# Experts' rows weighed at PSUM and scattered with accumulation onto the shared output, instead of gathered in a last stage

## Chip, cores and metric

One core of a Trainium2 chip. The metric is the device time of one execution in microseconds (us); the core has five engines (TensorE, VectorE, ScalarE, GpSimd, which the profile calls POOL, and SyncE or SP, which only issues DMAs), SBUF for tiles and PSUM for the results of matmuls. All data are fp32; matmuls take pairs of fp32r halves (high and low part), three products for one.

## The reference

4096 tokens of 512 features. A state-space scan gives x1; then come the experts, the part that matters here:

```
logits = xt @ gate_w ; probs = softmax(logits) ; top_p, top_i = top_k(probs, 2)
for k in 0, 1:                       # every token goes to two experts of 8
    pos = running count of the tokens of this expert and this k
    keep = pos < 640                 # tokens beyond 640 are dropped
    y = gelu(x @ w1[e] + b1[e]) @ w2[e] + b2[e] + gelu(x @ wd[e]) @ wu[e]
    out += y * keep * top_p[:, k]
sh = gelu(xt @ sw1 + sb1) @ sw2 + sb2 + gelu(xt @ swd) @ swu
out = x1 + layernorm(out + 0.2 * sh)
```

where xt is the layer-normalised x1, w1 is 512x2048 and w2 2048x512. The two experts of a token differ, so within one expert no token stands twice.

## The kernel before, in words

The program has four stages, with a barrier of all engines between them: `prepare`, `mix` (the scans; beside them the shared expert's output for 28 of the 32 tiles of 128 tokens, stored to sh_d), `experts` and `combine`.

`experts` (L1011) first does the shared expert's last four tiles beside the router. The router ends with 64 pairs of comparisons on VectorE (L1531, L1533) that TensorE multiplies into a table, slot_tok: which token stands in which of an expert's 1280 slots. An empty slot names token 0. Then 8 experts follow, each in three blocks of 2, 4 and 4 tiles of 128 slots (EB). A block has 17 steps j. In step j TensorE makes the hidden rows (`up(j)`, 12 matmuls to psH), ScalarE applies gelu, VectorE splits the result into hh and hl (L1413 to L1421), and TensorE multiplies these with W2 into psY (`down(j)`), always one step behind `up`. Step 0 is the low-rank part (L1, L2). At a block's end VectorE evicts psY with the bias b2 to yst (L1436), and only after that, its order being fixed, splits step 0 of the next block; `down(0)` waits for it (L1628). yst has two tiles, so the third eviction waits until the first is stored. SP stores the tiles to y_d (L1186), one row for each slot.

Beside this the rows of coming blocks are gathered by POOL with indirect DMAs (`gather`, L1339) from xt_d into two xrow tiles and turned by TensorE at steps 2, 6, 10 and 14 of the block before (FRONT). A gather waits until the turn of its tile two before (s_T). In an expert's third block the next expert's weights come in: SP loads 36 pieces through four raw tiles (L1159), ScalarE rounds each to its high part (`convert_chunk`, from step 2 on, L1238), POOL subtracts for the low part (`lows`, L1334), which frees the raw tile. The last pieces are done after the block has ended. The order on POOL is written out by hand: gathers of blocks 1 and 2, `slots` (a wait for the new indices), gathers of block 0 of the next expert, then its 36 `lows`. All of it is one in-order queue, as is each other engine's.

`combine` (L1695) takes the tokens in 16 groups of two tiles through a ring of six buffers. POOL gathers each token's two rows from y_d (64 indirect DMAs, L1740), SP loads sh_d and x1_d, ScalarE weighs the first row (L1751), VectorE adds the second and 0.2 times the shared row (L1777, L1782), takes the statistics (L1786, L1789) and the scale; ScalarE normalises (L1759), VectorE adds x1 (L1803), SP stores out (L1719).

Of the kernel before, what the change touches and what calls it, by code (L numbers as in the profile page):

```python
# [17 lines left out]
F32 = mybir.dt.float32  # L18
# [20 lines left out]
TG, NG = 2, NS // 2  # L39

# [333 lines left out]
def mix(nc, sem, const, early, x, dt_d, dtx_d, bc_d, xT_d, w, ws_d, lgT_d, x1_d, xt_d, sh_d):  # L374
# [6 lines left out]
    with ExitStack() as ctx:  # L381
# [49 lines left out]
        s_bias = sem("b_biases_in")  # L431
# [153 lines left out]
        def _(act):  # L585
# [94 lines left out]
            for g in range(END):  # L680
# [31 lines left out]
        def _(dve):  # L712
# [50 lines left out]
            def shared_out(b, t):  # L763
                dve.wait_ge(s_mm2, (b + 1) * J)
                dve.wait_ge(s_bias, 32)
# [4 lines left out]
                nc.vector.tensor_tensor(yst[t][:, :], psS[t][:, :], b2bc[:, :], ALU.add).then_inc(s_yev, 1)  # L770
# [237 lines left out]
TRAIL = 2  # L1008


def experts(nc, sem, const, w, ws_d, lgT_d, x1_d, xt_d, sh_d, y_d):  # L1011
# [7 lines left out]
    wgt, row_g, lg = const["wgt"], const["row_g"], const["lg"]  # L1019
    with ExitStack() as ctx:  # L1020
# [5 lines left out]
        L1h, L1l = sb("L1h", [P, DT, P], F32R), sb("L1l", [P, DT, P], F32R)  # L1026
        L2 = sb("L2", [L3, D], F32R)
        X = [(sb(f"X{n}h", [P, DT, r], F32R), sb(f"X{n}l", [P, DT, r], F32R)) for n, r in (("a", 512), ("b", 512))]
# [5 lines left out]
        yst = [sb(f"yst{q}", [P, D]) for q in range(2)]  # L1034
# [3 lines left out]
        graw = sb("graw", [P, DT, E])  # L1038
        rs1, nm1 = sb("rs1", [P, NT]), sb("nm1", [P, NT])
        slot_tok = sb("slot_tok", [P, E * ST])  # L1040
        idx = sb("idx", [P, ST], I32)
# [4 lines left out]
        U, ones = sb("U", [P, P], F32, rt), sb("ones", [P, P], F32, rt)  # L1046
        m8, r8, w8 = sb("m8", [P, NT], F32, rt), sb("r8", [P, NT], F32, rt), sb("w8", [P, E], F32, rt)
        mx, pos = sb("mx", [P, K, NT], F32, rt), sb("pos", [P, K, NT], F32, rt)
        tok, tok_f = sb("tok", [P, NT], I32, rt), sb("tok_f", [P, NT], F32, rt)

        count_i = RA[:, :, :, :].rearrange("p k t e -> p (k t e)").bitcast(I32)[:, 0:P]
        count_f = U

# [6 lines left out]
        X.append((sb("Xch", [P, DT, 256], F32R), sb("Xcl", [P, DT, 256], F32R)))  # L1060
# [13 lines left out]
        s_yst = [sem(f"c_y_stored{q}") for q in range(2)]  # L1074
# [27 lines left out]
        def expert(e, k):  # L1102
            o, n = EB[k]
            return dict(B=e * 3 + 1 + k, t0=e * ST + BT + o, th=e * (ST // 2) + (BT + o) // 2, n=n,
                        gathered=True)
# [40 lines left out]
        y_v = y_d.rearrange("(e j p) d -> e p j d", e=E, j=ST)  # L1146

        @block.sync
        def _(sp):
# [33 lines left out]
            def store(at, dest):  # L1183
                for t in range(at["n"]):
                    pass_gate(sp, s_yev, at["t0"] + t + 1, g_sp)
                    sp.dma_start(dest(t), yst[t % 2][:, :]).then_inc(s_yst[t % 2], 16)  # L1186

            def store_shared(b):
                store(shared(b), lambda t: sh_d[bass.ds(b * (BT * P) + t * P, P), :])
# [698 lines left out]
```

## Time and profile before

| | |
|---|---|
| three runs | 3653.09, 3645.42, 3647.03 us; median 3647.03 |
| profiled execution, its own time | 3653.11 us |
| its span, first to last instruction | 3651.4 us |
| mean granted clock of TensorE | 0.917 |
| TensorE busy | 3143.7 us, 86% |
| VectorE, ScalarE, POOL busy | 51%, 38%, 43% |
| bytes moved by DMA | 480.08 MB |
| stages by TensorE's work | mix to about 1430 us, experts to 3524, combine to the end |

Busy time is the time in which an engine has an instruction at work; matmuls overlap, so a matmul's own 0.39 us is more than its share of 0.23. An idle stretch is given in brackets ahead of an instruction, with what ended it. A landing is the moment at which the last of a DMA's 16 queues reports.

### The profile page before, as it was taken

What the parts mean: (1) busy time and instruction counts of PE and PEld (TensorE: products, weight loads), DVE (VectorE), ACT (ScalarE), POOL (GpSimd) and SP (SyncE); (2) the same over time, 40 slices, a digit from 0 to 9 for tenths busy, and PEclk for the clock granted to TensorE, in tenths of its full rate; (3) what the DMA queues carried; (4) which work ended last, traced back from release to release, by engine and by line L of the source; (5) the groups of instructions that cost most, each with busy time, mean ns of one, the idle gap of its engine ahead of it and who ended that gap; (6) DMA issues with size and microseconds to landing.
All of it is one profiled execution on the core that took longest, in us unless ns stands there. A gap on an engine that the chain in (4) does not pass through costs nothing. (4 is left out here: it accounts for less than half of the span.)

```text
span 3651.4 us, 45197 instructions
## 1 busy us (share of the span) xinstructions
PE 3143.7 (86%) x15190; PEld 2580.2 (71%) x15190; DVE 1856.8 (51%) x2762; ACT 1394.6 (38%) x2475; POOL 1583.1 (43%) x1459
## 2 busy tenths in 40 slices
PE   6445698988989987989999999999999999999960
PEld 3223477777777775778888888888888888888840
DVE  6489889998899881542232222222222222223238
ACT  7445576666766762311221312212213122131114
POOL 1067787978979873420320502304214033051025
PEclk8655699999999998979999999999999999999985
DMA  6848697796886946810321302203113022031039
GB/s 231 230 153 224 188 246 193 209 257 192 235 217 207 257 139 181 249 52 18 88 64 30 109 24 63 79 15 101 53 41 99 21 72 76 9 110 44 15 125 347
DMA packets 281672, 480.08 MB, mean 131 GB/s; under 512 B 30497, under 2 KB 106097, under 8 KB 281474
## 3 DMA queue, kind: packets, MB, share of 16 engines
q1 hardware_dynamic: 223104, 296.62, 27.9%
q0 software_dynamic: 56704, 180.38, 16.7%
q8 instruction: 133, 2.18, 0.2%
q10 hardware_dynamic: 1666, 0.36, 0.1%
q14 instruction: 65, 0.53, 0.0%
HBM read 380.18 MB, written 97.11 MB: 131 GB/s over the span
## 5 line engine op out<-in xcount | busy, mean ns | idle before, releaser
L1419 DVE CAST hh<-h 128x512 fp32r<-128x512 f32 (+1 forms) x400 | 159.2, 398 | 1301.5 <-ACT h L1271 1295.7
L1271 ACT ACTIVATE h<-c_psH,b1e 128x512 f32<-128x512 f32 (+1 forms) x384 | 237.2, 618 | 1356.2 <-PE c_psH L1590 1328.8
L818 POOL TENSOR_TENSOR u<-dtxs,Bt 128x512 f32<-128x512 f32 x512 | 667.3, 1337 | 168.6 <-DVE b_psA L722 145.2
L722 DVE TENSOR_TENSOR_SCAN b_psA<-b_psA,carry,u 128x512 f32<-128x512 f32 x512 | 657.0, 1283 | 61.5 <-ACT b_psA L595 56.4
L1339 POOL DMA_INDIRECT xrow<-xt_d,idx x80 | 89.2, 1116 | 1099.6 <-PE c_psT L1581 603.3
L1632 PE MATMUL c_psY<-W2h,hh 128*128 128x512 f32 x1344 | 534.3, 398 | 0.1
L926 PE MATMUL b_psY<-ident,pr 128*128 128x128 f32 x2048 | 343.5, 306 | 215.0 <-DVE pr L729 197.7
L1632 PE MATMUL c_psY<-W2h,hl 128*128 128x512 f32 x1344 | 526.0, 391 | 0.0
L1632 PE MATMUL c_psY<-W2l,hh 128*128 128x512 f32 x1344 | 525.4, 391 | 0.0
L926 PEld LDWEIGHTS b_psY<-ident,pr 128*128 128x128 f32 x2048 | 263.5, 155 | 299.5 <-DVE pr L729 247.3
L729 DVE TENSOR_TENSOR pr<-b_psA,Ct 128x512 f32<-128x512 f32 x512 | 354.3, 692 | 17.9 <-DMA Ct<-bc_d 0.2
L595 ACT ACTIVATE b_psA<-dts,A_neg 128x512 f32<-128x512 f32 x512 | 354.4, 692 | 16.1
L1334 POOL TENSOR_TENSOR W1l<-raw,W1h 128x512 fp32r<-128x512 f32 x128 | 204.7, 1599 | 294.4 <-ACT W1h L1238 294.2
L961 PE MATMUL b_psH<-Xh,w 128*128 128x512 f32 x896 | 318.1, 416 | 7.7 <-DMA w<-ws_d 7.7
L980 PE MATMUL b_psS<-w,hhs 128*128 128x512 f32 x896 | 295.2, 411 | 0.0
L1632 PEld LDWEIGHTS c_psY<-W2h,hl 128*128 128x128 f32 x1344 | 252.9, 188 | 54.8
L1632 PEld LDWEIGHTS c_psY<-W2h,hh 128*128 128x128 f32 x1344 | 253.7, 189 | 51.2 <-DVE hl L1421 4.2
L1632 PEld LDWEIGHTS c_psY<-W2l,hh 128*128 128x128 f32 x1344 | 253.6, 189 | 47.2 <-issue 0.2
L1421 DVE TENSOR_TENSOR hl<-h,hh 128x512 fp32r<-128x512 f32 (+1 forms) x400 | 246.7, 617 | 13.7
L1590 PE MATMUL c_psH<-Xbh,W1l 128*128 128x512 f32 x576 | 224.1, 389 | 0.0
L1590 PE MATMUL c_psH<-Xbh,W1h 128*128 128x512 f32 x576 | 224.1, 389 | 0.0
L1590 PE MATMUL c_psH<-Xbl,W1h 128*128 128x512 f32 x576 | 224.1, 389 | 0.0
(251 smaller groups left out, 5596.8 us busy)
## 6 DMA issues: line engine op xcount, KB each, us to landing
w<-ws_d POOLq DMA_DIRECT2D x224, 512.0 KB, 6.8
raw<-in_w SPq DMA_DIRECT2D x256, 256.0 KB, 2.8
Bt<-bc_d SPq DMA_DIRECT2D x64, 512.0 KB
Ct<-bc_d SPq DMA_DIRECT2D x64, 512.0 KB, 24.5
y_d<-yst SPq DMA_DIRECT2D x80, 256.0 KB
xn<-in_x SPq DMA_DIRECT2D x8, 1024.0 KB, 6.3
xT_d<-xnT SPq DMA_DIRECT2D x8, 1024.0 KB, 8.5
dt_d<-a_dt SPq DMA_DIRECT2D x8, 1024.0 KB, 9.5
```

The lines of the kernel that those rows point to most:

```text
L595: nc.scalar.activation(psA[g % 2][:, :], dts[s % 2][:, :], ACT.Exp, scale=A_neg[:, s % DT, n:n + 1]).then_inc(s_dA, 1)
L722: nc.vector.tensor_tensor_scan(psA[q][:, :], psA[q][:, :], u[g % U_RING][:, :], carry[:, k:k + 1], ALU.mult, ALU.add).then_inc(s_h, 1)
L729: nc.vector.tensor_tensor(pr[g % PR_RING][:, :], psA[g % 2][:, :], C_of(g), ALU.mult)\
L818: nc.gpsimd.tensor_tensor(u[g % U_RING][:, :], dtx[s % 2][:, :], Bt[n // TG][:, n % TG, :], ALU.mult)\
L926: last = nc.tensor.matmul(psY[:, t, :], pr[g % PR_RING][:, t * P:(t + 1) * P], ident[:, :], start=(n == 0 and t == 0), stop=False, is_tran ...
L961: last = nc.tensor.matmul(psH[:, :], a[:, d, :], v[:, d, :], start=(d == 0 and i == 0), stop=(d == DT - 1 and i == 2))
L980: last = nc.tensor.matmul(psS[t][:, :], a, v, start=False, stop=(j == FC and i == 2))
L1271: nc.scalar.activation(h32[:, 0:n * P], psH[j % 2][:, 0:n * P], ACT.Gelu, bias=b1[:, j - 1:j]).then_inc(s_gelu, 1)
L1334: nc.gpsimd.tensor_tensor(lo, view, hi.bitcast(F32), ALU.subtract).then_inc(s_wlo, 1)
L1421: nc.vector.tensor_tensor(hl[j % 2][a], h32[a], hh[j % 2][a].bitcast(F32), ALU.subtract)\
L1590: last = nc.tensor.matmul(out, a, b, start=(i == 0), stop=(i == n - 1))
L1632: last = nc.tensor.matmul(psY[t][:, :], a[j % 2][:, c], b, start=False, stop=(j == J - 1 and i == 2))
```

## The change

The last stage no longer gathers. The shared output, already times 0.2, is stored to acc_d instead of sh_d; each expert's rows, times their token's weight, are added onto acc_d by an indirect DMA that accumulates, 80 in all. `tail` takes `combine`'s place: it loads the sum and x1, normalises, adds, stores. For this:

- ScalarE prepares each yst tile with weight times b2 (`weigh_bias`, at steps 4, 6, 8, 10 of each block); the eviction is psY times the weight plus that. There are four yst tiles now; which block uses which, and when one is free again, is written in Y_TILE and Y_TURN. In an expert's first block tiles 0 and 1 come from the third and fourth scatter of the expert before.
- The weights are turned, stored to two columns in DRAM after the router, and gathered for each tile of slots, 128 of 4 bytes (`gather_weights`, POOL).
- Two tables instead of one: slot_g for gathers, slot_s for scatters, where an empty slot names a spare row of its own behind row 4096.
- POOL also stores the shared rows of the last block and issues the scatters. The first scatter of an expert waits for all those of the expert before, since two experts can have the same token; VectorE writes the new scatter indices at step 12 of the first block after the same wait.
- SP keeps only weights and b2.

```diff
+Y_TILE = ((0, 1), (2, 3, 0, 1), (2, 3, 0, 1))
+Y_TURN = ((0, 0), (0, 0, 1, 1), (1, 1, 2, 2))
+Y_USES = (3, 3, 2, 2)
+WEIGH_AT = (4, 6, 8, 10)
@@ mix: ScalarE, VectorE @@
+                if g == NU:
+                    act.wait_ge(s_bias, 32)
+                    nc.scalar.mul(b2bc[:, :], b2bc[:, :], SHARE).then_inc(s_b02, 1)
-                nc.vector.tensor_tensor(yst[t][:, :], psS[t][:, :], b2bc[:, :], ALU.add).then_inc(s_yev, 1)
+                nc.vector.scalar_tensor_tensor(yst[t][:, :], psS[t][:, :], SHARE, b2bc[:, :], ALU.mult, ALU.add)\
+                    .then_inc(s_yev, 1)
@@ experts: SP @@
             load_pieces(1, weights_of(0))
-            store_shared(SB - 1)
             bias2(0, expert(0, 0))
-            store_expert(0, 0)
-            store_expert(0, 1)
...
@@ experts: ScalarE @@
+            def weigh_bias(at, t):
+                if at["gathered"]:
+                    e, k = at["e"], at["k"]
+                    i, free = y_free(e, k, t)
+                    pass_gate(act, s_b2, (e + 2) * 16, g_act)
+                    pass_gate(act, s_wg[k], (e + 1) * EB[k][1] * 16, g_act)
+                    pass_gate(act, s_yst[i], free, g_act)
+                    scale = wsl[:, EB[k][0] + t:EB[k][0] + t + 1]
...
+                nc.scalar.mul(yst[i][:, :], b2bc[:, :], scale).then_inc(s_b2w, 1)
...
+            act.wait_ge(s_wT, 1)
+            nc.scalar.copy(weight_rows, psT[1][0:K * NT, 0, :]).then_inc(s_wTc, 1)
+            act.wait_ge(s_wTc, 1)
+            for k in range(K):
+                act.dma_start(w_d[k].rearrange("(r p) o -> r (p o)", p=P), weight_rows[k * NT:(k + 1) * NT, :])\
+                    .then_inc(s_wst, 16)
+            act.wait_ge(s_wst, K * 16)
@@ experts: POOL @@
+            def scatter(e, k):
+                at = expert(e, k)
+                if k == 0:
+                    pass_gate(pool, s_sidx, e + 1, g_pool)
+                    for i in range(4):
+                        pass_gate(pool, s_yst[i], added(e, i), g_pool)
+                for t in range(EB[k][1]):
+                    i = Y_TILE[k][t]
+                    pass_gate(pool, s_yev, at["t0"] + t + 1, g_pool)
+                    nc.gpsimd.indirect_dma_start(
+                        out=acc_d[:, :],
+                        out_offset=bass.IndirectOffsetOnAxis(ap=sidx[:, EB[k][0] + t:EB[k][0] + t + 1], axis=0),
+                        in_=yst[i][:, :], in_offset=None, bounds_check=T + SLOTS - 1,
+                        compute_op=ALU.add).then_inc(s_yst[i], 16)
...
             def steady(e, last=False):
-                for k in (1, 2):
-                    for t in range(EB[k][1]):
-                        gather(e, k, t)
...
+                gathers(e, 2, range(2))
+                scatter(e, 0)
+                gathers(e, 2, range(2, 4))
+                gather_weights(e, 2)
+                if not last:
+                    slots(e + 1)
+                    gathers(e + 1, 0, range(2))
+                    gather_weights(e + 1, 0)
+                scatter(e, 1)
+                if not last:
+                    for j in range(J):
+                        lows(e + 2, j)
+                    gathers(e + 1, 1, range(2))
+                scatter(e, 2)
+                if not last:
+                    gathers(e + 1, 1, range(2, 4))
+                    gather_weights(e + 1, 1)
@@ experts: VectorE @@
-                dve.wait_ge(s_b2, bias_count)
                 for t in range(n):
-                    after(dve, s_yst[t % 2], (at["th"] + t // 2) * 16)
-                    nc.vector.tensor_tensor(yst[t % 2][:, :], psY[t][:, :], b2bc[:, :], ALU.add).then_inc(s_yev, 1)
+                    dve.wait_ge(s_b2w, at["t0"] + t + 1)
...
+                    nc.vector.scalar_tensor_tensor(yst[i][:, :], psY[t][:, :], scale, yst[i][:, :], ALU.mult, ALU.add)\
+                        .then_inc(s_yev, 1)
...
+            def scatter_rows(e):
+                for i in range(4):
+                    pass_gate(dve, s_yst[i], added(e, i), g_dve)
+                v.tensor_copy(sidx[:, :], slot_s[:, bass.ds(e * ST, ST)]).then_inc(s_sidx, 1)
...
-                run(expert(e, 0), (e + 2) * 16, nxt=(expert(e, 1), X_OF[1]))
+                run(expert(e, 0), nxt=(expert(e, 1), X_OF[1]), extra={12: (lambda: scatter_rows(e),)})
@@ tail, in combine's place @@
+        @block.sync
+        def _(sp):
+            for g in range(NG):
+                sp.dma_start(y[g][:, :, :], rows(acc_d, g)).then_inc(s_y[g], 16)
+                sp.dma_start(x1r[g][:, :, :], rows(x1_d, g)).then_inc(s_x1[g], 16)
+        @block.gpsimd
+        def _(pool):
+            for g in range(NG):
+                pool.wait_ge(s_x, (g + 1) * G)
+                pool.dma_start(rows(out, g), y[g][:, :, :]).then_inc(s_out, 16)
+            pool.wait_ge(s_out, NG * 16)
```

In `tail` each of the 16 groups has its own tiles. ScalarE does the root and the normalising, VectorE `stats(g)`, `scale(g - 1)` and `residual(g - 2)` in turn, as before without the two weighted sums. The L1 tiles of step 0 have 104 columns now instead of 128, and some tiles of the router share space with one of the X tiles. VectorE gets four small operations on 80 columns after the router's table, one of them ahead of the indices.

## Rows read from the trace of the kernel before

**Rows 1.** Busy us by stretch, expert stage: engines, granted clock, DMA share, GB/s

```profile
1560.00:3524.00 1964.00, 1923.86 (x9300) 1622.40 (x9299) 541.48 (x1139) 422.09 (x755) 441.92 (x340) 0.98 0.18 55
```

**Rows 2.** The same view, last stage: the whole, and its middle

```profile
3531.00:3651.40 120.40, 0.00 (x0) 0.00 (x0) 87.27 (x192) 48.48 (x81) 75.81 (x64) 0.50 0.94 349
3535.00:3630.00 95.00, 0.00 (x0) 0.00 (x0) 72.29 (x159) 39.40 (x66) 71.27 (x61) 0.50 1.03 382
```

**Rows 3.** Lines of the last stage, VectorE: busy us, mean ns | idle before

```profile
L1777 DVE SCALAR_TENSOR_TENSOR d_y<-d_y,wgt 128x512 f32<-128x512 f32 x32 | 22.7, 749 | 31.1 <-ACT d_y L1751 16.3 <-DMA d_y<-y_d,row_g 14.3 <-issue 0.5
L1782 DVE SCALAR_TENSOR_TENSOR d_y<-d_sh,d_y 128x512 f32<-128x512 f32 x32 | 20.6, 685 | 0.0
...
L1786 DVE BATCH_NORM_STATS2 d_st<-d_y 128x6 f32<-128x512 f32 x32 | 20.4, 680 | 0.0
```

**Rows 4.** Waits of the expert stage: us in total, times, longest us

```profile
PE c_psY L1628 <- DVE hh L1416: 19.9, 9, 2.9
...
DVE yst L1436 <- DMA y_d<-yst: 31.8, 15, 3.2
```

**Rows 5.** DMA issues: KB each, median us from issue to landing

```profile
xrow<-xt_d,idx POOLq DMA_INDIRECT x80, 3.8
...
xt_d<-xrow SPq DMA_DIRECT2D x4, 256.0 KB, 2.0
```

**Rows 6.** Timeline of the seam before the last stage, and its end

```profile
3524.11 1.29 DVE L1436 TENSOR_TENSOR yst<-c_psY,b2bc 128x512 f32<-128x512 f32 x2 [3.49 <-PE c_psY L1632]
...
3527.02 1.29 DVE L1436 TENSOR_TENSOR yst<-c_psY,b2bc 128x512 f32<-128x512 f32 x2 [1.62 <-DMA y_d<-yst]
3531.05 0.38 SPq L1724 DMA_DIRECT2D d_sh<-sh_d  x1
...
3645.33 2.49 DVE L1803 TENSOR_TENSOR d_y<-d_y,d_x 128x512 f32<-128x512 f32 x4
```

**Rows 7.** Timeline of two turns to a new expert, engine by engine: start, us

```profile
1850.81 1.29 DVE L1436 TENSOR_TENSOR yst<-c_psY,b2bc 128x512 f32<-128x512 f32 x2 [2.53 <-DMA y_d<-yst]
...
1852.66 0.42 DVE L1416 TENSOR_TENSOR hh<-h,hl 32x256 fp32r<-32x256 f32 x1
...
1853.13 0.73 PE L1628 MATMUL c_psY<-L,hh 96*128 96x512 f32 x2 [2.38 <-DVE hh L1416]
...
1852.24 1.01 POOL L1339 DMA_INDIRECT xrow<-xt_d,idx  x1 [0.30 <-issue]
...
1849.67 0.38 ACT L1265 ACTIVATE h<-c_psH 96x256 f32<-96x256 f32 x1 [0.17 <-ACT b1e L1312]
...
1862.94 0.47 ACT L1271 ACTIVATE h<-c_psH,b1e 128x256 f32<-128x256 f32 x1 [2.15 <-PE c_psH L1590]
1865.78 0.47 ACT L1271 ACTIVATE h<-c_psH,b1e 128x256 f32<-128x256 f32 x1 [2.36 <-PE c_psH L1590]
...
3291.40 0.42 DVE L1416 TENSOR_TENSOR hh<-h,hl 32x256 fp32r<-32x256 f32 x1
...
3288.90 0.38 ACT L1265 ACTIVATE h<-c_psH 96x256 f32<-96x256 f32 x1
```

**Rows 8.** Busy us by stretch behind two turns; TensorE's gap at the second

```profile
1853.00:1860.00 7.00, 6.87 (x37) 6.20 (x38) 1.51 (x5) 1.25 (x3) 0.25 (x1) 0.76 0.57 181
1999.00:2006.00 7.00, 6.36 (x29) 5.06 (x28) 3.30 (x6) 2.32 (x6) 3.38 (x4) 1.00 0.60 173
...
1999.89 1.20 PE L1628 MATMUL c_psY<-L,hh 96*128 96x512 f32 x4 [0.64 <-issue]
```

**Rows 9.** Timeline of VectorE after the shared block

```profile
1571.06 1.32 DVE L1436 TENSOR_TENSOR yst<-c_psY,b2bc 128x512 f32<-128x512 f32 x2 [1.58 <-DMA sh_d<-yst]
```

**Rows 10.** Timeline from the end of a second block to POOL's first lows

```profile
1993.95 1.29 DVE L1436 TENSOR_TENSOR yst<-c_psY,b2bc 128x512 f32<-128x512 f32 x2 [3.66 <-PE c_psY L1632]
...
2004.88 1.60 POOL L1334 TENSOR_TENSOR L1l<-raw,L1h 128x192 fp32r<-128x192 f32 x2 [2.84 <-ACT L1h L1238]
```

More of the change, by code:

```diff
@@ L39 @@
 TG, NG = 2, NS // 2
+SHARE = 0.2
 def after(eng, sem, value):
@@ L1033, in experts @@
         xrow = [sb(f"xrow{q}", [P, D]) for q in range(2)]
-        yst = [sb(f"yst{q}", [P, D]) for q in range(2)]
+        yst = [sb(f"yst{q}", [P, D]) for q in range(4)]
         b2bc = sb("b2bc", [P, D])
@@ L1181, in rows @@
                     row_out(b, t)
[L1183 to L1189, printed above, removed]
-            def store_expert(e, k):
-                store(expert(e, k), lambda t: y_v[bass.ds(e, 1), :, EB[k][0] + t, :].rearrange("o p d -> (o p) d"))
             def bias2(e, at):
-                pass_gate(sp, s_yev, at["t0"], g_sp)
+                pass_gate(sp, s_b2w, at["t0"], g_sp)
                 sp.dma_start(b2bc[:, :], w["b2"][bass.ds(e, 1), :].rearrange("o d -> (o d)").partition_broadcast(P))\
@@ L1276, in run @@
                         extra[j]()
+                    if j in WEIGH_AT and WEIGH_AT.index(j) < n:
+                        weigh_bias(at, WEIGH_AT.index(j))
                     if wset is not None and j >= TRAIL:
@@ L1376, in _ @@
                 pool.wait_ge(s_xts[q], BT // 2 * 16)
+            store_shared(SB - 1)
             slots(0)
-            for t in range(EB[0][1]):
-                gather(0, 0, t)
-            def steady(e, last=False):
-                for k in (1, 2):
-                    for t in range(EB[k][1]):
-                        gather(e, k, t)
-                if last:
-                    return
-                slots(e + 1)
-                for t in range(EB[0][1]):
-                    gather(e + 1, 0, t)
-                for j in range(J):
-                    lows(e + 2, j)
+            gathers(0, 0, range(2))
+            pool.wait_ge(s_wst, K * 16)
+            gather_weights(0, 0)
+            gathers(0, 1, range(4))
+            gather_weights(0, 1)
+            def steady(e, last=False):
+                gathers(e, 2, range(2))
[15 more added lines that the diff above has]
+                    gather_weights(e + 1, 1)
             with pool.Fori(0, E - 1) as e:
@@ L1522, in expert_slots @@
                 pass_gate(dve, s_T, expert(e, 0)["t0"], g_dve)
[L1523 removed]
+                if not (isinstance(e, int) and e == 0):
+                    pass_gate(dve, s_wg[2], e * EB[2][1] * 16, g_dve)
+                v.tensor_copy(idx[:, :], slot_g[:, bass.ds(e * ST, ST)]).then_inc(s_idx, 1)
+            def scatter_rows(e):
+                for i in range(4):
+                    pass_gate(dve, s_yst[i], added(e, i), g_dve)
+                v.tensor_copy(sidx[:, :], slot_s[:, bass.ds(e * ST, ST)]).then_inc(s_sidx, 1)
             def find_slots():
@@ L1808, in _ @@
+            for g in range(NG + 2):
+                if g < NG:
+                    stats(g)
+                if 1 <= g <= NG:
                     scale(g - 1)
```

221 lines of the change are left out of this document (105 added, 116 removed).

## Prediction, made before the change was run

> **What bounds the kernel now.** I read the page first (TensorE busy 86% of the span), then busy time by stretch, the lines, waits and timelines of the last two stages. TensorE is busy 1923.9 of the 1964 us of the expert stage [rows 1]: there only what makes it wait counts. In the last 120.4 us it does nothing. That stage moves 120.4 us x 349 GB/s = 42.0 MB, with the DMA engines 0.94 busy over the whole and full, at 382 GB/s, from 3535 to 3630 [rows 2]. So the last stage is bound by bytes. Its arithmetic is less: VectorE has 87.3 us of work there [rows 2], 43.3 of it the two weighted sums [rows 3].
>
> In the expert stage TensorE waits for little, but for one thing repeatedly: 19.9 us in nine waits for hh of a block's first step, where VectorE is late. VectorE is late because after two evictions into its two yst tiles it waits for the stores: 31.8 us in 15 waits [rows 4].
>
> **The change, part by part.**
>
> *Last stage.* Bytes after: 16 groups x 3 transfers (sum, x1, out) x 0.524 MB = 25.2 MB. At 382 GB/s [rows 2] that is 65.9 us. Loads need no buffer, so SP issues all 32 at once, and the engines stay fed; stores go out on POOL's queue and share them. First bytes I put 1.7 us after the first issue, a little under the 2.0 us in which a plain store of 256 KB lands [rows 5]. The last y lands with about three stores (1.6 MB, 4.1 us) still to move. Behind it lie two statistics of 0.68 us [rows 3], about 1 us of small operations, two normalisations, which I give the 0.75 us of the longest row of that size [rows 3], a last residual of 0.6 us [rows 6], 0.4 us for handing over, and the last store, 3.6 us: from the last residual's end at 3647.8 [rows 6] to that of the span. That is 8.5 us. Sum: 1.7 + 65.9 - 4.1 + 8.5 = 72.0 us against 120.4: **-48.4 us**. VectorE keeps 87.3 - 43.3 = 44.0 us of work, under the 65.9, so it does not become the bound. The slow bound of the rate is the 349 GB/s of the whole stage (+6.3 us); a faster one than 382 is not to be had with the engines at 1.03 busy, but for some 3 us by the spread of its parts.
>
> The rate that I use comes from the row. The Trainium skill (HBM Reference, Specifications) gives a core about 358 GB/s as its share and about 425 when it streams alone; by these figures the 25.2 MB would take an estimated 70.4 or 59.3 us. The row lies between.
>
> *Seam before the last stage.* Now: last eviction pair at 3527.02 after a 1.6 us wait for a store, first load of the last stage at 3531.05, so 6.9 us from the first eviction [rows 6]. After: four tiles, so four evictions run through to 3526.8. The fourth scatter starts at about 3528.9: the first when the first eviction is done, 3524.9, then one each 1.33 us, the pitch of POOL's indirect DMAs (1.01 busy, 0.30 between [rows 7]). Landing: a gather takes 3.8 us from issue [rows 5]; an accumulating scatter is in no row. Below it can't be under the 2.0 us of a plain store [rows 5]; above, if each of the 8 rows that a queue gets (128 over 16) is read, added and written before the next begins, it is 8 x 2.0 = 16 us. I take 5 to 6 us, near the gather, which also has 128 rows of 2 KB picked by index. First load then at 3535, hence **+3 us**.
>
> *Turns from an expert to the next (7).* At 1847 VectorE's second pair starts at 1850.81 instead of 1848.3, after 2.5 us of waiting; hh is done at 1853.08, 1.0 us behind the evictions' end, and TensorE goes on after a gap of 2.38 us [rows 7]. With four tiles the next limit is ScalarE's gelu, which ends at 1850.05: hh at 1851.1, a gain of 1.9. At 3286 the same reading (gelu ends at 3289.28, hh at 3291.82 [rows 7]) gives 1.4. The seven, of which these are the first and the last, sum to **-13.7 us**. Behind the gap TensorE's granted clock falls from 2.4 to 1.2 GHz for a while: over 7 us its mean is 0.76, so 1.7 us are lost [rows 8]. Behind a gap of 0.64 us it stays at 1.00 [rows 8]. The new gaps are 0.45 to 0.7 us in six turns, so I take the dip away in six: **-10 us**.
>
> *Turns from the second to the third block (8).* VectorE's wait is the same there, TensorE's gap 0.49 to 0.65 us (0.64 in the row of [rows 8]); gelu is done early, so all goes: **-4.8 us**.
>
> *Router.* VectorE's wait of 1.58 us for the store of the shared rows stands directly ahead of its 128 comparisons, which TensorE waits for [rows 9]; one small operation is added before the indices: **-1.3 us**. Transposing, copying and storing the weights lies beside those comparisons (27 us); if that cover went, it would be some 6 us once.
>
> *POOL.* It gets 80 scatters and 80 weight gathers, 160 x 1.33 = 213 us on an engine with 441.9 us of work in 1964 [rows 1]. The order decides. Ahead of a new set's lows stand two gathers, two weight gathers and four scatters, which end some 15 us after the second block; the lows start 11 us after it now, at 2004.9 for a block whose evictions began at 1993.95 [rows 10]. These 4 us reach ScalarE's next conversion as a wait of some 2 us, in a step where it idles over 3 us, and are made up within two steps; if they weren't, gelu would be late by the rest. At the turn the order is: last lows, two gathers (to 1853.25 [rows 7]), four scatters, and only then the later gathers, not needed before step 10. SP loses its stores and waits for nothing new.
>
> *ScalarE.* 84 multiplications of some 0.7 us (the size of rows 3), at steps 4 to 10. It idles over 2 us a step even in the short block [rows 7], so their time is hidden; their wait is not necessarily. In an expert's first block the one at step 4 needs yst tile 0 back, the third of the four scatters: issued at 1853.55 + 2 x 1.33 = 1856.2, landed like a gather at 1860.0. gelu of step 4 is at 1862.94 now [rows 7] and, with the 1.9 and the 1.7 us gained ahead of it, at 1859.3; gelu of step 5 is 2.84 us behind. The multiplication may start until 1861.4 without delaying it, and TensorE has another 1.4 us (a down-product) before it starves. So a landing within 5.2 us of issue costs nothing, within 6.6 nothing on TensorE. I allow 0.5 us in each turn: **+3 us**. Should the scatter be later, queued behind the stalled multiplication are the gelus, behind them VectorE's splits and all of TensorE.
>
> VectorE's step 12, where it now waits for the last expert's scatters before it writes the new row indices, is over 35 us into the block: nothing, unless a scatter takes 16 us. The evictions read PSUM as before, 0.69 us [rows 6]. The bias of the mix stage: one multiplication, beside the scans: nothing.
>
> The Trainium skill (DMA: Bandwidth & Descriptors, Rules for kernel authors) says that nothing holds the bytes between an accumulate's read and its write, so an earlier one must be waited for. That is the rule that speaks against this change, since it puts waits into VectorE's and POOL's order; no run here shows its price yet.
>
> **Sum:** -48.4 + 3 - 13.7 - 10 - 4.8 - 1.3 + 3 = -72 us. The profiled execution took 3653.1 us around its span of 3651.4; less 72, 3581. The three runs before have a median of 3647.0, 6.1 lower, so I predict **3575 us**.
>
> **Rivals.**
> (a) *The turns give nothing.* The accumulating scatters land 9 to 10 us after issue, and follow each other more slowly than POOL issues them. Then the multiplication at step 4 waits some 4 us, TensorE about 3, in 7 turns 21 us, and the seam costs 5 more: 3647 - 72 + 26 = 3601. For: a read comes before each write. Against: at 2 KB a row the engines move 256 KB in 0.7 us.
> (b) *The last stage is slower than its bytes*, by its stores from POOL's queue between the loads: at 318 GB/s, a sixth under the rate of the row, 13 us more: 3588.
> (c) *Slower than before.* The rows of a scatter go one after the other and each scatter holds POOL's DMA queue, 16 us by the upper bound. The third lands 48 us after 1853.6; ScalarE stands at step 4 for 40 us and for some 10 more at step 6, in each of 7 turns: +350 us, with the seam +58, over 3950 us in all. It decides from about 6 us a scatter: three of them then hold step 4 up by some 10 us, which in 7 turns and the seam eats the 72. Against: gathers from the same queue show none of it, with the same rows; for: no row has an accumulating DMA.
> (d) *The edit doesn't do what it says*, the step-4 wait taking yst's place exactly, so that only the last stage counts: 3647 - 45 = 3602; its chance is in (a).
>
> **How the numbers follow.** Forecast 0.55, own range 3562 to 3590 (rate bounds -3 and +6, clock dips all gone -2 or all left +10). (a) 0.2, (b) 0.1, (c) 0.06; 0.09 for something between the forecast's range and no change, or below it. The range of 3560 to 3618 takes in the forecast, (a) and (b). No change would be within 0.2%, about what a measurement of this kernel can tell. Faster 0.91, same 0.03, slower 0.06.
>
> **What would show it.** Last stage: no indirect DMA, about 72 us, over 370 GB/s. Turns: no wait of VectorE's eviction for a store, TensorE's gap under 1 us, granted clock 1.00 behind it. ScalarE: no wait for yst at step 4. DMA issues: scatters landing after 5 to 6 us. I am wrong if ScalarE's multiplication waits over 2 us for a scatter, if the dip in the clock stays at short gaps, or if the last stage's rate falls under 350 GB/s.

## The result, and the profile after

The changed kernel took 3619.45 us (median of 4 runs, 3617.52 to 3623.88), the kernel before, run beside it, 3646.23: a ratio of 0.9921, 95% interval 0.9906 to 0.9935. The gain is 27 us where 72 were forecast, and the time lies 1.5 us above the range. The profiled execution took 3623.9 us around a span of 3622.1, 29.3 us under that of before.

By stretch of the changed kernel (us, busy time and count of PE, PEld, DVE, ACT, POOL, granted clock, DMA share, GB/s), the expert stage and, whole and middle, the last one:

```profile
1570.00:3536.00 1966.00, 1923.77 (x9265) 1607.83 (x9264) 571.30 (x1149) 469.57 (x831) 635.83 (x496) 0.98 0.24 54
3552.00:3622.10 70.10, 0.00 (x0) 0.00 (x0) 46.54 (x128) 28.68 (x49) 11.76 (x16) 0.50 0.94 359
3560.00:3610.00 50.00, 0.00 (x0) 0.00 (x0) 38.02 (x108) 23.88 (x42) 9.55 (x13) 0.50 1.05 403
```

Against [rows 2] the last stage is 50.3 us shorter (120.4 to 70.1), against [rows 1] the expert stage gained nothing. Its end and the seam, from the timeline:

```profile
3536.24 2.72 DVE L1514 SCALAR_TENSOR_TENSOR yst<-c_psY,slot_weights,yst 128x512 f32<-128x512 f32 x4 [3.50 <-PE c_psY L1727]
...
3537.84 1.56 POOL L1405 DMA_INDIRECT acc_d<-yst,sidx  x1 [83.30 <-DVE yst L1514]
3539.70 1.56 POOL L1405 DMA_INDIRECT acc_d<-yst,sidx  x1 [0.30 <-issue]
...
3543.43 1.56 POOL L1405 DMA_INDIRECT acc_d<-yst,sidx  x1 [0.31 <-issue]
...
3552.03 0.39 SPq L1817 DMA_DIRECT2D d_y<-acc_d  x1
```

The four evictions run through, as forecast, but the first load comes 15.8 us after they begin, against 6.9 in [rows 6]: +8.9 us. The waits of the expert stage (us in total, times, longest):

```profile
ACT W1h L1242 <- DMA raw<-in_w: 59.7, 15, 6.6
...
PE c_psY L1723 <- DVE hh L1492: 16.0, 5, 3.6
ACT b1e L1339 <- issue: 14.7, 6, 2.5
...
PE c_psY L1723 <- issue: 6.4, 2, 3.4
...
PE c_psY L1727 <- DVE hl L1497: 4.4, 5, 1.3
```

VectorE's wait for a store [rows 4] is gone, yet TensorE still waits 22.4 us ahead of L1723 (16.0 + 6.4; it was 19.9 + 3.6 ahead of L1628). New is the row of b1e: six times ScalarE stands some 2.5 us with nothing to wait for.

I measured blocks from the start of a block's evictions to that of the next block's. Sums over all blocks of a kind, us:

| blocks | before | after | forecast | difference |
|---|---|---|---|---|
| shared to the first (router) | 93.9 | 91.6 | -1.3 | -2.3 |
| second blocks, 8 | 740.1 | 752.7 | 0 | +12.6 |
| third blocks, 8 | 739.2 | 739.9 | -4.8 | +0.7 |
| turns to the next expert, 7 | 382.7 | 382.0 | -23.7 +3 | -0.7 |
| expert stage | 1955.9 | 1966.2 | -26.8 | +10.3 |

With the last stage's -50.3, the seam's +8.9 and +1.8 ahead of the expert stage that makes the span's -29.3. So most of the mis-forecast is in the expert stage: 37 us, in three places, none of them a wait for a scatter; 6 us are in the seam.

These are sums of one execution each. In e7 and e11 below, which leave the time of the kernel before as it is, the seven turns sum to 379.4 and 376.6 us and the router's block takes 92.9 us in both: a difference of some 6 us in the turns, or of 1 us in the router, can be chance. The second and third blocks repeat within 0.4 us a sum.

### The profile page after: what moved, and what is told of

It reads as the page before. It is cut to its first block and busy times, and to the rows that moved or that the text cites. A ratio compares the mean times of both kernels' runs of the same rounds, so it can differ in the third digit from the quotient of the medians.

```text
span 3622.1 us, 45551 instructions
## 1 busy us (share of the span) xinstructions
PE 3161.7 (87%) x15191; PEld 2578.5 (71%) x15191; DVE 1848.0 (51%) x2708; ACT 1426.5 (39%) x2529; POOL 1724.7 (48%) x1576
## 5 line engine op out<-in xcount | busy, mean ns | idle before, releaser
L1495 DVE CAST hh<-h 128x512 fp32r<-128x512 f32 (+1 forms) x400 | 170.6, 426 | 1290.2 <-ACT h L1289 1245.0
L733 DVE TENSOR_TENSOR pr<-b_psA,Ct 128x512 f32<-128x512 f32 x512 | 354.0, 691 | 19.2 <-DMA Ct<-bc_d 1.6
L1361 POOL TENSOR_TENSOR W1l<-raw,W1h 128x512 fp32r<-128x512 f32 x128 | 193.4, 1511 | 263.5 <-ACT W1h L1242 263.3
L1497 DVE TENSOR_TENSOR hl<-h,hh 128x512 fp32r<-128x512 f32 (+1 forms) x400 | 257.6, 644 | 13.7
```

The costliest lines, as they stand in the source:

```text
L733: nc.vector.tensor_tensor(pr[g % PR_RING][:, :], psA[g % 2][:, :], C_of(g), ALU.mult)\
L1361: nc.gpsimd.tensor_tensor(lo, view, hi.bitcast(F32), ALU.subtract).then_inc(s_wlo, 1)
L1497: nc.vector.tensor_tensor(hl[j % 2][a], h32[a], hh[j % 2][a].bitcast(F32), ALU.subtract)\
```

## Experiments

Ratios are to the kernel before, run beside each; its medians there were 3649 to 3653 us, so ratios and profiles are compared, not medians.

### Where Xa starts: e1, e2, e7, e11, e15

All eight second blocks are 1.57 us longer, without a wait. They are the ones that read Xa, and of the products with W1 only Xa's are slower. Lines by form, first the kernel before, then the changed one (mean ns):

```profile
L1590 PE MATMUL c_psH<-Xah,W1h 128*128 128x512 f32 x512 | 199.2, 389 | 0.0
```

```profile
L1684 PE MATMUL c_psH<-Xah,W1h 128*128 128x512 f32 x512 | 201.8, 394 | 0.0
L1684 PE MATMUL c_psH<-Xbh,W1h 128*128 128x512 f32 x516 | 200.9, 389 | 0.0
```

Their pitch, from the starts of some 150 such matmuls in a row in the timeline, went from 0.2267 to 0.2332 us; 204 of them in a block are 1.3 us. The change moved Xa in SBUF, from 160 to 96 bytes past a multiple of 256 in each partition; the weights are at 160 in both.

```diff
+        sb("pad", [P, 16])          # e1, changed kernel: ahead of Xa
+        sb("pad", [P, 48])          # e2, kernel before: ahead of Xa, 192 bytes
+        sb("pad0", [P, 48])         # e11, kernel before: ahead of W1h, all tiles move
```

> The changed kernel with 64 bytes of padding ahead of Xa, so that Xah and Xal begin 160 bytes past a multiple of 256 in a partition, as in the kernel before, instead of 96; they stay at the far end of SBUF. The eight second blocks took 94.08 us from first eviction to first eviction where the kernel before took 92.50. Theory A (what costs is where Xa starts against a multiple of 256, beside the weights' starts): the second blocks fall to 92.5 us, 8 x 1.57 = 12.6 us less in all, some 3607 us, ratio to the kernel before near 0.989. Theory B (the far end of SBUF costs, not the start): the blocks stay at 94.1 and the time at 3619, ratio 0.992. Theory C (other traffic in these blocks costs: the scatters, ScalarE's extra products): stays at 94.1 too.

> The kernel before with Xah and Xal moved by 192 bytes, from 160 to 96 past a multiple of 256; every other tile keeps its phase. Theory A: its second blocks rise from 92.5 to about 94.1 us, 12.6 us in all, some 3659 us, ratio 1.0035. Theories B and C: nothing moves, ratio 1.000.

e1: 0.9898 (0.9883 to 0.9912); second blocks 92.63 us, pitch 0.2266. e2: 1.0024 (1.0015 to 1.0033), less than the 1.0035 expected, though the second blocks rose as expected, to 94.06, pitch 0.2331. The cost can be given to the old kernel and taken from the new by the start of one tile: theory A; traffic and the far end of SBUF are out.

> The kernel before with 96 bytes of padding ahead of W1h: both weights' tiles, L1, L2, Xa, Xb, hh, hl and raw now all begin at a multiple of 256 bytes instead of 160 past it; Xc goes from 32 to 128 past it. Theory A1 (the start against a multiple of 256 or 128 alone decides, and 0 is no worse than 160): second and third blocks at 92.5 us or less; if a clean start is better than 160, each matmul of 512 columns falls below its pitch of 0.227 us, towards 0.213 us, which would be 92.5 x 0.94 = 87 us a block. Theory A2 (what costs is the distance between the start of the moving tile and that of the weights, 0 here and in the kernel before, 64 in the changed one): exactly 92.5 us, no change, ratio 1.000.

> The kernel before with 192 bytes of padding ahead of W1h: the weights, Xa, Xb, hh and the rest all begin 96 bytes past a multiple of 256. Theory A1 (a start at 96 is itself what costs): pitch of all matmuls of 512 columns with a moving Xa or Xb at 0.233 us, second and third blocks at 94.1 us, 16 x 1.55 = 25 us slower, ratio 1.007. Theory A2 (the distance of 64 bytes between the moving tile's start and the weights' start, counted against 256, costs; here it is 0): 92.5 us, ratio 1.000.

e7 (96 bytes ahead of W1h): 1.0004 (0.9995 to 1.0014), second blocks 92.54, Xa 0.2264. e11: 1.0003 (0.9993 to 1.0013), 92.52, 0.2264. With weights and Xa together at 0, at 96 or at 160 nothing changes. So it is a distance between starts (A2), not the start. That it is the distance to the weights is argued, not shown: e1, e2 and e15 moved the X tiles against every other tile of the stage, too, and the weights are named because they are the other operand of these matmuls. A start at a multiple of 256 gave no faster pitch, as A2 has it.

> The kernel before with Xa 128 bytes, Xb 64 bytes and Xc 64 bytes past the weights' start counted against 256 (0, 0 and 128 before; the changed kernel had 192 for Xa and Xc). If only a distance of 192 costs, all pitches stay: 0.2267 for Xa and Xb, 0.119 for Xc. If every distance that is no multiple of 128 costs, Xb goes to 0.233 us and third blocks to 94.1 us, with Xa at 0.2267. If every distance but 0 costs, both do, and the kernel is 25 us slower.

```diff
+        sb("pad", [P, 32])          # Xa 128 bytes on
+        sb("pad2", [P, 48])         # Xb 64 on in all
+        sb("pad4", [P, 48])         # Xc, with pad3 of 48 ahead of h32
```

One run, 3667.2 us, 14 us over the median of the kernel before where 25 were expected; its second and third blocks are 21 us longer together. Pitches in us by distance past the weights' start, modulo 256:

| moving tile | 0 | 64 | 128 | 192 |
|---|---|---|---|---|
| Xa, Xb (512 columns) | 0.2267 | 0.2305 | 0.2329 | 0.2332 |
| Xc (256 columns) | 0.1193 | 0.1181 | 0.1195 | 0.1170 |

For 512 columns every tried distance but 0 costs. Xc does not follow that: it is fastest at 192. I have no rule that gives both rows. Xc had moved with the change as well, from 128 to 192, and so its matmuls are faster than before: some 0.5 us in each first block (204 x 0.0025), which nobody forecast.

### POOL's order: e4

In the third blocks the low parts of the weights wait for the scatters. POOL's timeline of the changed kernel, in the block that begins at 1997.75:

```profile
2001.57 1.01 POOL L1366 DMA_INDIRECT xrow<-xt_d,idx  x1 [52.46 <-issue]
...
2004.20 1.11 POOL L1390 DMA_INDIRECT slot_weights<-w_d,idx  x1 [0.30 <-issue]
...
2006.93 1.63 POOL L1405 DMA_INDIRECT acc_d<-yst,sidx  x1 [0.30 <-issue]
...
2013.63 2.27 POOL L1361 TENSOR_TENSOR L1l<-raw,L1h 128x192 fp32r<-128x192 f32 x2
```

They start 15.9 us into the block ([rows 10]: 10.9), as forecast. But the wait was not made up: ScalarE waits for raw up to 6.6 us and TensorE on hl.

```diff
-                if not last:
-                    slots(e + 1)
-                    gathers(e + 1, 0, range(2))
-                    gather_weights(e + 1, 0)
-                scatter(e, 1)
+                scatter(e, 1, range(2))
+                if not last:
+                    slots(e + 1)
+                    gathers(e + 1, 0, range(2))
+                scatter(e, 1, range(2, 4))
...
                     for j in range(J):
                         lows(e + 2, j)
+                    gather_weights(e + 1, 0)
```

> The changed kernel with POOL's order alone changed: of the second block's four scatters two are issued at once, ahead of the gathers of the next expert, two behind them, and the next expert's row weights are gathered after the low parts. The low parts of the weights began 15.9 us into the third block (10.9 before the change). Theory A (POOL's queue delays the low parts, these hold the raw buffers, and ScalarE's h comes late): low parts begin at 10 to 11 us, TensorE's gaps on DVE hl in the third blocks (4.4 us in all) go, and ScalarE's waits for raw at its casts fall from 59.7 to about 17 us: 4 us less, 3615 us. Theory B (these gaps hide each other): below 1 us.

0.9903 (0.9888 to 0.9918). Low parts at 11.3 to 12.0 us, the third blocks 91.77 us each, ScalarE's wait for raw at W1h 27.9 us, hl 1.6 us. Against the kernel before the third blocks are now 6 us shorter together, the 4.8 forecast and a little more: the gain had been there and was covered.

### ScalarE at the loop back: e3, e5, e6, e12, e16, e17

ScalarE's timeline at the turn of 2089.90, and the 6 us from the moment at which TensorE goes on, with its granted clock:

```profile
2091.89 0.63 ACT L1242 CAST W2h<-raw 128x512 fp32r<-128x512 f32 x1 [0.72 <-DMA raw<-in_w]
2095.03 0.20 ACT L1339 COPY b1e<-b1T 128x16 f32 x1 [2.52 <-issue]
2095.40 0.38 ACT L1283 ACTIVATE h<-c_psH 96x256 f32<-96x256 f32 x1 [0.17 <-issue]
```

```profile
2097.06:2103.06 6.00, 6.00 (x20) 5.32 (x21) 1.81 (x4) 0.95 (x2) 5.09 (x4) 0.50 0.86 133
```

In the kernel before, b1e followed the last cast at once. It is late only in the six turns that the loop makes, not in the seventh, which stands behind the loop in the program. ScalarE's instruction queue, which the page lists as q14, went from 65 packets to 93.

> The kernel before with 50 semaphore increments, which nothing waits for, added to ScalarE's loop over the experts: its body grows from 280 to 330 instructions; the change made it 328. Theory A (a body of this length is fetched again at each loop back, and ScalarE stands for it): in the six turns inside the loop ScalarE now stands some 2.4 us before its first instruction of the new expert, the instruction queue of ScalarE shows about 93 packets instead of 65, and TensorE's gap ahead of L1628 grows by about 0.5 to 1 us in those turns; in the whole 3 to 8 us slower, ratio 1.001 to 1.002. Theory B (the stall came from the waits of the new ScalarE instructions, not from the length): 65 packets, no stall, ratio 1.000.

1.0014 (1.0005 to 1.0023), 96 packets: increments that nothing waits for bring the stall and the packets. They cost only some 5 us here, for in the kernel before VectorE's wait for a store [rows 7] holds the same turns up beside it.

```diff
-                    pass_gate(act, s_b2, (e + 2) * 16, g_act)
-                    pass_gate(act, s_wg[k], (e + 1) * EB[k][1] * 16, g_act)
-                    pass_gate(act, s_yst[i], free, g_act)
+                    if k == 0 and t == 0:
+                        pass_gate(act, s_b2, (e + 2) * 16, g_act)
+                    if t == 0:
+                        pass_gate(act, s_wg[k], (e + 1) * EB[k][1] * 16, g_act)
+                    act.wait_ge(s_yst[i], free)
```

> The changed kernel with fewer semaphore instructions around ScalarE's products of bias and row weight: the waits for the bias row and for the row weights once in a block, the wait for the free tile on the product itself. ScalarE's loop body has 302 instructions instead of 328 (280 before the change). Theory A (the body's length sets how much is fetched again): packets of ScalarE's instruction queue between 65 and 93; if the stall at the loop back needs the longer body, it shrinks or goes. Theory B (any length over that of the kernel before has the full stall): about 90 packets and the 2.4 us stall in six turns stay.

> The changed kernel with the experts' products of bias and row weight made on VectorE instead of ScalarE, at the same chunks; ScalarE's body is 280 instructions again, VectorE's grows from 209 to 238. Theory A (length of ScalarE's body): 65 packets in ScalarE's instruction queue, b1e follows the last cast of W2h at once, as before the change, and the block from third to second eviction at the turns gets 0.5 to 1 us shorter in six turns: 3 to 6 us, 3614 to 3616 us. Theory B (ScalarE stands there for another reason): no change. Against A's gain: VectorE's own products may delay hh and hl where they fall, 0.3 us each.

```diff
+                nc.vector.tensor_scalar(yst[i][:, :], b2bc[:, :], scale, None, ALU.mult).then_inc(s_b2w, 1)   # e6
```

e5: 0.9859 (0.9845 to 0.9873), 63 packets. e6: 0.9867 (0.9853 to 0.9882), 64 packets. Both lose the stall, and the turns fall to 50.6 to 52.2 us. That is far more than the 3 to 6 us that e6's text expected: the expert stage is 21 us shorter in e5 and 23 in e6 than in the changed kernel. The 6 us behind TensorE's gap in the same turn of e5:

```profile
2089.57:2095.57 6.00, 6.00 (x40) 5.54 (x41) 2.21 (x6) 1.97 (x4) 4.78 (x5) 1.00 0.70 149
```

Ahead of `down(0)` TensorE stood 3.0 to 3.6 us in the changed kernel's six turns inside the loop and 2.2 us in the seventh, and its granted clock over the next 6 us was 0.50 to 0.72 in six of the seven; in e5 it stood 1.1 to 1.5 us in the six of the loop, and the clock stayed at 1.00 (2.4 GHz), and 2.2 us in the seventh, with 0.72 behind it. So the stall cost its own time and the clock as well.

> The kernel before with 40 semaphore increments in ScalarE's loop over the experts, body 320 instructions. 302 (e5) left ScalarE's instruction queue at 63 packets, 328 and 330 (the change, e3) had 93 and 96. Either about 65 packets and the short turns (the bound lies between 320 and 328) or about 95 and b1e some 2.4 us late in six turns (between 302 and 320).

One run, 3654.4 us: 95 packets, with b1e late in six turns. Lengths of 280 and 302 are free, 320 and up are not. That looked like a bound on length, and was not:

```diff
+            for _ in range(80):     # e16, ahead of the loop; e17: 45, in the kernel before
+                act.sem_inc(g_act, 1)
```

> The changed kernel with 80 semaphore increments put into ScalarE's stream ahead of its loop over the experts, while it waits for VectorE's comparisons; the loop body keeps its 328 instructions and all else is the same. Theory L (the body's length causes the stall at the loop back): about 93 packets in ScalarE's instruction queue, turns of 55 us, 3619 us, ratio 0.992. Theory P (where the body lies against blocks of 256 instructions in the stream: it must end inside the block behind the one in which it begins): e5, e12 and the change bound the old start at 201 to 210 instructions into a block; 80 more put it 25 to 34 into the next one, so that 328 fit, and the stall goes: 65 packets, turns of 51 us, 3600 us, ratio 0.987. The Trainium skill (Runtime: NRT & Kernel Launch, Instruction fetch mechanics) states what theory P says: blocks of 256 instructions, two of them held, and a taken branch to outside them waits for a fetch.

> The kernel before with 45 semaphore increments ahead of ScalarE's loop over the experts; its body keeps its 280 instructions. Theory L: nothing, 65 packets, ratio 1.000. Theory P: the body now begins 237 to 246 instructions into a block and ends past the second, so the stall appears as in e3: about 95 packets, ScalarE some 2.4 us late at b1e in six turns, ratio 1.001 to 1.002.

e16: 0.9857 (0.9840 to 0.9873), the body still 328 long:

```profile
q14 instruction: 64, 0.52, 0.0%
```

e17: 1.0008 (0.9998 to 1.0017), the body still 280 long, 95 packets, and ScalarE at a turn:

```profile
2091.35 0.62 ACT L1238 CAST W2h<-raw 128x512 fp32r<-128x512 f32 x1 [0.66 <-DMA raw<-in_w]
2094.54 0.20 ACT L1314 COPY b1e<-b1T 128x16 f32 x1 [2.56 <-issue]
```

Eighty instructions more make the changed kernel faster, 45 more bring the stall to the old one (its time is within the interval of no change; the stall and the packets are not in doubt). Theory L is out. What counts is where the body lies in the stream. The Trainium skill (Runtime: NRT & Kernel Launch, Instruction fetch mechanics) has it so: "A taken branch whose target isn't in the current 2-page window forces a DMA fetch of the target page before execution can continue". The packets, 64 and 95, agree; how long a page is, no run here measured.

### The scatter itself: e8

```diff
-                        in_=yst[i][:, :], in_offset=None, bounds_check=T + SLOTS - 1,
-                        compute_op=ALU.add).then_inc(s_yst[i], 16)
+                        in_=yst[i][:, :], in_offset=None, bounds_check=T + SLOTS - 1).then_inc(s_yst[i], 16)
```

> The changed kernel with its scatters writing instead of adding: the sum over the experts is left out of the computation, the rows and queues are the same. Theory A (the addition in DRAM is what makes a scatter dear): the four last scatters take much less than the 3 us of all DMA engines each that their 256 KB took, the first load of the last stage comes 8 to 10 us after the last eviction starts instead of 15.8, and the span falls by 5 to 7 us; POOL still takes 1.56 us for each. Theory B (POOL's descriptors and the scattered rows set it, not the addition): first load still 14 to 16 us after the eviction, and the time stays at 3619.

0.9887 (0.9872 to 0.9901). The scatters in the tile view of acc_d, the changed kernel's and e8's (duration in ns, minimum/median/maximum):

```profile
L1405 POOL DMA_INDIRECT acc_d<-yst,sidx x80: 1547/1578/1778, 1663.3 to 3543.4; - x80
```

```profile
L1405 POOL DMA_INDIRECT acc_d<-yst,sidx x80: 980/998/1154, 1663.1 to 3531.1; - x80
```

The changed kernel's trace has no landing for its scatters, but e1, e4, e5, e14 and e16 scatter in the same way and have it. From the DMA issues of e16, then of e8, the median from issue to landing:

```profile
acc_d<-yst,sidx POOLq DMA_INDIRECT x80, 5.3
```

```profile
acc_d<-yst,sidx POOLq DMA_INDIRECT x80, 2.9
```

And the two seams by stretch, the changed kernel's and e8's:

```profile
3536.00:3552.00 16.00, 0.21 (x1) 0.00 (x0) 2.72 (x4) 0.00 (x0) 6.23 (x4) 0.64 0.53 66
```

```profile
3525.40:3537.40 12.00, 0.17 (x1) 0.00 (x0) 2.73 (x4) 0.00 (x0) 3.93 (x4) 0.69 0.23 87
```

Adding costs 0.58 us more of POOL for each scatter (1.58 against 1.00, where no difference was expected) and 2.4 us more until it lands, and its transfer takes the 16 DMA engines 2.1 us (16 x 0.53 / 4) instead of 0.7 (12 x 0.23 / 4). The seam is 12.0 us instead of 15.8, a smaller gain than the 5 to 7 us expected, and third blocks fall to 91.77, as in e4.

Even plain, the seam is 5 us over that of before. What it waits for stands in the views of the block's end (L1029) of the changed kernel, for SP and for POOL, and of e8 for POOL: start in us, behind the durations in ns.

```profile
L1029 SPq DRAIN  x1: 7/7/7, 3549.3 to 3549.3; - x1
L1029 POOLq DRAIN  x1: 12189/12189/12189, 3539.6 to 3539.6; - x1
```

```profile
L1029 POOLq DRAIN  x1: 8397/8397/8397, 3529.0 to 3529.0; - x1
```

SP has waited for the last scatter and is through at 3549.3, less than 6 us after that began at 3543.4. But POOL, too, ends its block, with a DRAIN that lasts to 3551.8, and the first load follows 0.3 us behind it. In e8 it lasts to 3537.4 and the load comes at 3537.6. In the kernel before, POOL has nothing to drain there. So some 2.5 us of the changed kernel's seam lie behind the landing and come with issuing the last scatters from POOL; no run moved them, so this rests on the traces.

### All together: e9, e10, e13, e14

> The changed kernel with three of its side costs taken out together: Xa at 160 bytes past a multiple of 256 (e1), POOL's order (e4), ScalarE's body at 302 instructions (e5). If the three are separate and each works as read: from the shared block's eviction to that of the last block 91.5 for the first, 8 x 92.6, 7 x 91.8 + 90.8 for the third blocks, and 7 x 50.7 for the turns, 1920.6 us instead of 1966.2, so 45.6 us less: 3574 us, ratio 0.979. If they hide each other (POOL or the loads of the raw weights bound the shorter turns), the third blocks stay at 93 us and it comes to 3585.

0.9863 (0.9847 to 0.9880), where 0.979 was expected: second blocks 92.62, third 91.75, ScalarE's queue 64 packets, but the turns at 54 us again. A new wait had come up. ScalarE's, of e9:

```profile
ACT yst L1276 <- DMA acc_d<-yst,sidx: 32.2, 7, 5.2
```

and in its timeline, the scatter having been issued at 2095.81:

```profile
2102.00 0.72 ACT L1276 ACTIVATE yst<-b2bc,slot_weights 128x512 f32<-128x512 f32 x1 [5.18 <-DMA acc_d<-yst,sidx]
```

That is the wait of the forecast's rival (a), at 6.2 us from issue rather than 9 to 10. In the changed kernel it is 1.6 us in all, for ScalarE comes late to it. But the short body alone does not make it dear. In e5 it is

```profile
ACT yst L1275 <- DMA acc_d<-yst,sidx: 19.2, 7, 4.0
```

and the turns take 50.6 to 52.2 us. The rest comes from e4's order, which puts two gathers of row weights ahead of the last four scatters: in e9 the third of them starts 13.2 to 13.5 us into the turn, in e5 10.5 to 10.8. So e4's edit gives in the third blocks and takes in the turns. Besides, e9 has Xc back at distance 0, 0.5 us slower in each turn.

> As e9, and the last stage issues its 16 loads of x1 ahead of its wait for the last scatters, then those of the sum. The scatters of the last block left all DMA engines with some 100 GB/s for 8 to 10 us. If they can share that time: 8 MB come at some 400 GB/s beside the wait, and the stage ends 6 to 9 us earlier than in e9, 3566 us. If the loads slow the scatters down as much, or the sum's loads behind them in the queue start the pipeline late: no gain, up to 5 us slower.

0.9893 (0.9876 to 0.9909), 11 us slower than e9, a miss: up to 9 us faster or 5 slower was expected. The loads of x1 began at 3531.47, again 15.4 us after the eviction, though SP's own wait for the scatters was gone. What held them is POOL's DRAIN at the end of the block, of 11.8 us, to 3531.2:

```profile
L1029 POOLq DRAIN  x1: 11817/11817/11817, 3519.4 to 3519.4; - x1
```

So x1 could not come beside the scatters. And with all x1 ahead of the sum, VectorE's 45.6 us of work began 25.6 us into the stage and ran full (9.9 us of 10 from 3575 on); the stage took 78.6 us instead of 70.1.

```diff
+WEIGH_0 = (12, 14)
...
+                    when = WEIGH_0 if n == 2 else WEIGH_AT
+                    if j in when:
+                        weigh_bias(at, when.index(j))
```

> e9 with one more edit: in an expert's first block, whose chunks are half as long, the two products of bias and row weight come at chunks 12 and 14 instead of 4 and 6, some 25 us later, when the four scatters of the block before have landed. Theory A (the wait for their landing, 5.2 us at its longest, is what held e9's turns at 54 us): ScalarE's wait for acc_d falls from 32 to below 5 us, TensorE's wait on DVE hl (9.5 us) goes, the turns take 50.7 us, and the time is 3574 to 3578 us, ratio 0.980, within a few us of the forecast of 3575. Theory B (something else bounds the turn): 3595 to 3600.

> As e13, with Xc ahead of Xa, so that Xc begins 64 bytes before the weights' start counted against 256 (as in the changed kernel, where its matmuls of 256 columns had a pitch of 0.1170 us) and Xa with it (0.2267 us). In e9 both had distance 0, and Xc 0.1193 us. If the distance acts on each tile as read, with opposite sign for the two shapes: the eight first blocks get 204 x 0.0023 = 0.47 us shorter each, 4 us less than e13. If Xc's pitch came from something else (the clock, other traffic): as e13.

e13: 0.9824 (0.9807 to 0.9840), turns 52.1 to 52.9 us, the wait for acc_d gone from ScalarE's list. That is theory A, but not its size: 50.7 us a turn and a ratio of 0.980 were expected, and the rest was not tracked down. e14: 0.9810 (0.9796 to 0.9825), turns 51.4 to 52.4 us, Xc's pitch 0.1169 instead of 0.1191, 5.5 us less than e13 where 4 were expected. e14 is the fastest of these kernels, 1.1% under the changed one. Its expert stage is 1926.9 us, 29.1 under that of before; the forecast had 26.8. Its ratio is that of the forecast (3575 / 3646.2 = 0.9805), in part by luck: against the forecast it has 5.5 us more in the seam, and less in the last stage (2.1), the third blocks (1.3) and the router (1.2); and of the 21.5 us by which its turns are shorter, some 3.5 come by Xc's pitch, which was in no sum.

## Why the prediction was wrong

- **Last stage: right.** 70.1 us against 72.0 forecast, at 403 GB/s in the middle against the 382 used.
- **Seam: mis-sized**, +8.9 for +3. The landing was right: 5 to 6 us taken, 5.3 measured (e16). What was wrong: the first scatter starts 1.6 us behind the first eviction (0.8 taken), and POOL's pitch was a gather's, 1.33 us, where an adding scatter has 1.86; together 2.4 us by the fourth. POOL's DRAIN behind the landing, some 2.5 us, was in no term. And the sum is off in itself: a first load at 3535 after 3531.05 is +3.9, not +3. e8 shows that the addition makes up 3.8 us of the seam.
- **Turns to the next expert: the step failed.** "With four tiles the next limit is ScalarE's gelu, which ends at 1850.05" was read from a trace in which ScalarE's loop body lay well in the stream; with the change it lay badly (e16, e17), and gelu came some 2.5 us later in six turns. The clock's fall stayed for the same reason: it follows TensorE's gap, as the forecast said. The step costed ScalarE's 84 products as busy time and left out their instructions. With the stall taken away by e16 and nothing else, the seven turns sum to 359.5 us, 23.2 under before, where the forecast has 23.7. That the two agree so well is in part luck. TensorE's seven gaps ahead of `down(0)` fell from 18.7 to 9.3 us together, 9.4 less where 13.7 were forecast: they are 1.05 to 1.35 us in the six turns, not 0.45 to 0.7. One reason stands in the rows of a turn, of the kernel before and of e16:

```profile
2091.57 0.28 DVE L1413 CAST hh<-h 64x256 fp32r<-64x256 f32 x1
```

```profile
2083.01 0.96 DVE L1491 CAST hh<-h 64x256 fp32r<-64x256 f32 x1 [0.56 <-ACT h L1283]
```

VectorE's first split, now early enough to fall beside POOL's last subtraction, takes 0.77 to 0.96 us instead of 0.28; no run shows that POOL is the cause. What made up for it is some 3.5 us by Xc's pitch (7 x 0.5), which was in no term, and the clock. It stayed at 1.00 in the six turns, as forecast, and by the granted clock over the seven turns an estimated 12 us came back (13.7 us lost before, 1.7 in e16) where 10 were forecast.

- **Second blocks: not in the forecast at all.** +12.6 us by a tile's start that the diff moves without naming it.
- **Third blocks: the sum's cover did not hold.** The 4 us that the low parts lose "are made up within two steps" was wrong; they ate the 4.8 us. The alternative stood in the same sentence, unpriced. With e4's order the gain is 6.0 us.
- **Router: right** within what one execution shows, -2.3 for -1.3. **ScalarE's waits, +3:** ScalarE waited 1.6 us in the changed kernel; the mechanism is real but hidden by the stall (19.2 us of waiting in e5, 32.2 in e9).
- **Rivals.** (a) and (d) gave times nearer to the result than the forecast, 3601 and 3602, by a mechanism that was not at work. (c) is out: a scatter lands after 5.3 us and takes 2.1 us of the DMA engines, and the wait it feared was 5.6 us at its longest (e10). (b) is out.

The 37 us of the expert stage: turns 23.0, second blocks 12.6, third blocks 5.5, less 1.0 of the router and the 3 allowed. The experiments account for each, and e14 has them back in sum.

## What to carry to other kernels

Of an edit that adds instructions to a loop, count them, and compare the packets of the engine's instruction queue: if they jump, shorten the body or move it, even by idle instructions ahead of the loop. Of an edit that adds or drops a tile, list where every matmul operand begins before and after. And when a stall goes, look for the wait that it had hidden (here the scatter's landing) before judging the next edit. Where an engine has issued the last DMAs of a block, look at its DRAIN before moving loads ahead.

## What the runs showed of the hardware

- The pitch of a float32r matmul of 512 columns was 0.2267 us where the moving tile's start and that of the weights agree modulo 256 bytes (at 0, 96 and 160 alike), and 0.2305 to 0.2332 (up to 2.9% more) at the three other distances tried; with 256 columns 0.1170 to 0.1195, in another order.
- A loop body of 328 instructions ran without a stall and one of 280 with one, by its place in the stream; the stall was 2.2 to 2.9 us for each pass.
- An accumulating indirect scatter of 128 rows of 2 KB took 1.58 us of POOL against 1.00 plain, landed after 5.3 us (median) against 2.9, and took three times the DMA engines' time.
- At the end of a block, POOL's DRAIN lasted about 2.5 us beyond the landing of its last scatter (3.6 us with plain ones), and the next block's first load on SP came 0.25 us behind it.
